# A decoder layer on one core: x is loaded turned and raw, the mean is taken out of the weights once, and GpSimd makes the two halves of x

## The reference, cut to what matters

```python
x   = x + self_attention(layernorm(x))        # x: 32 tiles of 128 tokens x 512, 16 heads of 32, RoPE, causal
x   = x + cross_attention(layernorm(x), ctx)  # queries and output through an int8 rounding per token
out = x + experts(layernorm(x))               # 64 experts, top 8, at most 128 rows each
# layernorm: (x - m) / sqrt(v + eps), over the 512 features, without gain or bias
# self attention: q = rope(xn @ Wq.T + bq), k likewise, v = xn @ Wv.T + bv; one 128 x 128 causal block per head
```

## Time and profile before

| | |
|---|---|
| median of 3 runs | 1784.66 us |
| profiled execution | 1771.08 us, its span 1769.2 us |
| PE, DVE, ACT, POOL busy | 84%, 66%, 55%, 38% of the span |
| mean granted TensorE clock | 0.918 of full speed |
| setup, up to the third body | 0 to 55 us |
| pipeline | 55 to some 1300 us |
| experts | some 1300 to 1769 us |

### The profile page before, as it was taken

How to read it: one execution, slowest core, us unless ns; L and a number is a source line. 1 busy time by engine, 2 the same in 40 slices (tenths; PEclk the granted TensorE clock), 3 DMA queues, 4 the chain that set the end, 5 groups by cost and what they waited for, 6 DMA issues and landing times.

```text
span 1769.2 us, 36416 instructions
## 1 busy us (share of the span) xinstructions
PE 1480.6 (84%) x11380; PEld 1111.3 (63%) x11380; DVE 1165.4 (66%) x3111; ACT 966.9 (55%) x3345; POOL 674.6 (38%) x654
## 2 busy tenths in 40 slices
PE   3699988888898888988888888888872988887895
PEld 2577766666666666766666666666651655555564
DVE  6788776777777777767767777776762444444453
ACT  3477665666666666666666666666661433333342
POOL 0114333333334333433333433333343355444465
PEclk9899999998999999999899999999985999999997
DMA  9752222221110101000001010100049799999974
GB/s 299 285 203 97 90 90 101 100 85 61 44 40 28 36 24 30 24 24 24 24 24 30 24 32 27 30 24 19 19 133 331 209 274 273 278 247 301 267 132 50
DMA packets 159930, 196.01 MB, mean 111 GB/s; under 512 B 39733, under 2 KB 121909, under 8 KB 159872
## 3 DMA queue, kind: packets, MB, share of 16 engines
q1 hardware_dynamic: 120960, 157.47, 27.1%
q0 software_dynamic: 38912, 37.87, 10.5%
HBM read 127.80 MB, written 130.29 MB: 146 GB/s over the span
## 4 chain that ended last, share of the span: by engine, by line
DVE 25%; PE 22%; DMA 20%; issue 14%; another core or an unknown queue 12%; ACT 5%; POOL 1%; DVEq 1%; SPq 0%; POOLq 0%
DMA out<-x,slots 18%; PE bank L513 11%; PE bank L519 4%; DVE small L1250 3%; ACT probs L980 3%; PE bank L541 3%; DVE xn L1269 2%; DVE wide_a L1319 2%; DVE small L1283 2%; PE bank L495 2%; DVE small L1273 1%; DVE x L1325 1%; DVE x L1450 1%; DVE wide_b L1493 1%
## 5 line engine op out<-in xcount | busy, mean ns | idle before, releaser
L980 ACT ACTIVATE probs<-bank,small 128x128 f32<-128x128 f32 x1024 | 364.2, 384 | 155.5 <-DVE small L1283 152.1
L1732 POOL TENSOR_TENSOR small<-small,half 128x1 f32<-128x1 f32 x96 | 54.6, 568 | 721.5 <-DVE small L1255 719.9
L1767 POOL DMA_INDIRECT routed<-row,slots x248 | 252.9, 1020 | 132.6 <-issue 72.9
L1836 POOL DMA_INDIRECT out<-x,slots x128 | 200.1, 1563 | 202.2 <-DMA out<-x,slots 148.5
L1283 DVE TENSOR_REDUCE small<-bank 128x4 f32<-128x512 f32 x256 | 166.9, 684 | 133.1 <-remote 125.1
L980 ACT ACTIVATION_READ_ACCUMULATOR probs<-bank,small 128x1 f32 x1024 | 228.6, 223 | 0.0
L974 ACT ACTIVATE probsT<-bank 128x512 f32<-128x512 f32 x256 | 144.0, 610 | 84.3 <-PE bank L541 81.9
L541 PE MATMUL bank<-idf,probs 128*128 128x128 f32 x1024 | 160.4, 293 | 3.9 <-ACT probs L980 3.9
L541 PEld LDWEIGHTS bank<-idf,probs 128*128 128x128 f32 x1024 | 130.5, 152 | 35.4 <-issue 6.5
L513 PE MATMUL bank<-w_q_hi,xT_hi 128*128 128x512 f32 x128 | 73.5, 575 | 79.3 <-DVE xatt L1299 35.7
L1687 DVE TENSOR_SCALAR slots<-pairs 128x1 uint32<-128x1 f32 x128 | 13.7, 149 | 189.3 <-DMA out<-x,slots 182.9
(11 more groups left out here) (242 smaller groups left out, 3982.5 us busy)
## 6 DMA issues: line engine op xcount, KB each, us to landing
w_gate_up<-in_w_gate SPq DMA_DIRECT2D x128, 192.0 KB
w_gate_up<-in_w_up SPq DMA_DIRECT2D x128, 192.0 KB
w_down<-in_w_down SPq DMA_DIRECT2D x128, 192.0 KB
routed<-empty_row SPq DMA_DIRECT2D x16, 1280.0 KB, 10.1
x_in<-in_x SPq DMA_DIRECT2D x32, 256.0 KB, 2.6
ctx_sb<-in_ctxT_in SPq DMA_DIRECT2D x32, 256.0 KB, 3.0
x_res<-in_x SPq DMA_DIRECT2D x32, 256.0 KB, 2.6
out<-x SPq DMA_DIRECT2D x32, 256.0 KB
```

The costliest lines, as they stand in the source:

```text
L980: last = act.activation(probs[:, g, j * P:(j + 1) * P], bank[:, b, j * P:(j + 1) * P], ACT.Exp, bias=negated[:, h:h + 1], **({"accum_out": ...
L1732: pool.tensor_tensor(c["r0"], c["v"], half[:, :], ALU.pow).then_inc(g_pow[kind], 1)
L1767: pool.indirect_dma_start(routed, bass.IndirectOffsetOnAxis(ap=slots_of(m)[:, k:k + 1], axis=0), row_of(m)[:, :], None, bounds_check=SLOTS ...
L1836: pool.indirect_dma_start(out.rearrange("b p (h c) -> (b p h) c", h=2), bass.IndirectOffsetOnAxis(ap=place_of[k % 2][:, half_:half_ + 1], ...
```

## The change

- A copy of x that is already turned (`xT_in`, each tile as four blocks of 128 x 128 side by side) is a further input. SP loads it for each tile into xn (`load_turned_x`), behind `load_x`, when GpSimd has split the tile before.
- GpSimd makes both halves: `turned_x_hi` casts xn to xT_hi and `turned_x_lo` subtracts. Both stand in its body behind the power of the cross norm and ahead of that of the self norm. They are of raw x, neither centred nor scaled.
- TensorE's `turn_x`, ScalarE's `x_hi`, VectorE's `self_normed` and `x_lo` are gone.
- The mean: for q, k and v TensorE adds up the 512 input rows of the staged weight with a matrix of ones (4 matmuls of 128 x 512 in fp32 each), and VectorE takes 1/512 of it from the staged weight (`centre`), before it is split. Done once, in the setup.
- The scale 1/sqrt(v + eps) of a token is applied behind the projections: to v by ScalarE in `copy_values`, to q and k by VectorE as a factor in the last step of `rotate`. The order in `rotate` is now: both sine products, the cosine product, their sum, and then sum times scale plus turned bias.
- The statistics and the scale are made one body later (for tile cur-1 and cur-2), so `load_x` waits for the statistics of the tile before and no longer for its normed x.

```diff
             def load_x(m):
-                reached(sp, d_ln["self"], m - 1, 7, 7)
+                reached(sp, d_ln["self"], m - 1, 6, 1)
                 sp.dma_start(x_in[:, :], x[tile(m)]).then_inc(s_x_in, 16)
+
+            def load_turned_x(m):
+                reached(sp, g_xT, m - 1, 2, 2)
+                sp.dma_start(xn[:, :], xT_in[tile(m)]).then_inc(s_xT, 16)
...
             def queries_a(m):
-                reached(pe, a_xT, m, 1, 1)
+                reached(pe, g_xT, m, 2, 1)
...
-                if has(cur - 1):
-                    turn_x(cur - 1)
...
-            pe.wait_ge(s_ident, 16)
+            pe.wait_ge(s_init, 2)
+            for n, b in enumerate((2, 3, 6)):
+                pe.wait_ge(s_wload[n], 16)
+                for t in range(KT):
+                    last = pe.matmul(bank[:, b, :], ones_f, STAGE[n][:, t, :], start=(t == 0), stop=(t == KT - 1))
+                last.then_inc(p_mean, 1)
...
-                copy(v_sb[:, :], bank[:, 6, :], e_v)
+                reached(act, d_ln["self"], m, 6, 6)
+                act.activation(v_sb[:, :], bank[:, 6, :], ACT.Copy, scale=ln["self"]["r"]).then_inc(e_v, 1)
...
-                act.wait_ge(s_wload[n % 4], 16 * (n // 4 + 1))
+                if n < 3:
+                    act.wait_ge(d_centred, n + 1)
+                else:
+                    act.wait_ge(s_wload[n % 4], 16 * (n // 4 + 1))
...
-                until(dve, d_rope, nth(m, 5, 2))
-                dve.tensor_tensor(rot, rot, turned_bias[:, :], ALU.add).then_inc(d_rope, 1)
+                until(dve, d_rope, nth(m, 5, 3))
+                dve.tensor_tensor(rot, rot, roped[:, :], ALU.add).then_inc(d_rope, 1)
                 until(dve, d_rope, nth(m, 5, 4))
-                dve.tensor_tensor(roped[:, :], roped[:, :], rot, ALU.add).then_inc(d_rope, 1)
+                dve.scalar_tensor_tensor(out=roped[:, :], in0=rot, scalar=ln["self"]["r"], in1=turned_bias[:, :],
+                                         op0=ALU.mult, op1=ALU.add).then_inc(d_rope, 1)
...
             body(1)
+            centre(0, 2)
+            centre(1, 3)
             weights_lo(0)
+            centre(2, 6)
             weights_lo(1)
...
+            def turned_x_hi(m):
+                reached(pool, s_xT, m, 16, 16)
+                reached(pool, p_v, m - 1, 3, 3)
+                apart(pool)
+                pool.tensor_copy(flat(xT_hi), xn[:, :]).then_inc(g_xT, 1)
+
+            def turned_x_lo(m):
+                reached(pool, g_xT, m, 2, 1)
+                pool.tensor_tensor(flat(xT_lo), xn[:, :], flat(xT_hi).bitcast(F32), ALU.subtract).then_inc(g_xT, 1)
```

More of the change, by code:

```diff
@@ L272, in layer @@
         d_ln = {k: sem(f"dve_ln_{k}") for k in ln}
-        d_xT, d_rope = sem("dve_xT"), sem("dve_rope")
+        LN_STEPS = {"self": 6, "cross": 7, "ffn": 7}
+        d_rope = sem("dve_rope")
+        d_centred = sem("weights_centred")
         d_max, d_norm, d_xmax = sem("dve_max"), sem("dve_normed_probs"), sem("dve_xmax")
@@ L407, in body @@
                     load_x(cur)
+                if has(cur):
+                    load_turned_x(cur)
                 if has(cur - 2):
@@ L432, in _ @@
                 fill(part)
+            load_turned_x(3)
             load_x(4)
@@ L437, in _ @@
             load_residual(2)
+            load_turned_x(4)
             for part in range(9, 12):
@@ L890, in turn_quantised_weights @@
                 last.then_inc(s_wT, 1)
+            pe.wait_ge(s_init, 2)
[4 more added lines that the diff above has]
+                last.then_inc(p_mean, 1)
+            body(1)
             pe.wait_ge(s_ident, 16)
-            body(1)
             pe.wait_ge(s_lo_dve, 3)
+            body(2)
             pe.wait_ge(s_init, N_INIT)
-            body(2)
             turn_quantised_weights()
@@ L1051, in copy_cross_keysT @@
                 last.then_inc(e_xkT, 1)
[L1053 to L1056, removed]
             def exp_1(m):
@@ L1442, in rotate @@
                     reached(dve, p_k, m, 3, 3)
+                    reached(dve, d_ln["self"], m, 6, 6)
                 rotate_pairs(4, m)
@@ L1527, in body @@
             def body(cur):
-                if has(cur - 1):
-                    self_rsqrt(cur - 1)
+                if has(cur - 2):
+                    self_rsqrt(cur - 2)
                 if has(cur - 5):
@@ L1557, in body @@
                     cross_max_3(cur - 4)
-                if has(cur - 1):
-                    self_normed(cur - 1)
                 if has(cur - 3):
@@ L1575, in body @@
                     shares(cur - 5)
-                if has(cur):
-                    self_statistics(cur)
+                if has(cur - 1):
+                    self_statistics(cur - 1)
                 if has(cur - 5):
@@ L1591, in body @@
                     cross_average(cur - 4)
-                if has(cur - 1):
-                    x_lo(cur - 1)
                 if has(cur - 2):
@@ L1616, in weights_lo, with centre @@
                                   ALU.subtract).then_inc(s_lo_dve, 1)
+            def centre(n, b):
+                dve.wait_ge(p_mean, n + 1)
+                dve.scalar_tensor_tensor(out=STAGE[n][:, :, :], in0=bank[:, b, :].unsqueeze(1).to_broadcast([P, KT, D]),
+                                         scalar=-1.0 / D, in1=STAGE[n][:, :, :],
+                                         op0=ALU.mult, op1=ALU.add).then_inc(d_centred, 1)
             body(1)
+            centre(0, 2)
+            centre(1, 3)
             weights_lo(0)
+            centre(2, 6)
             weights_lo(1)
@@ L1759, in self_power @@
             def self_power(m):
-                reached(pool, d_ln["self"], m, 7, 3)
+                reached(pool, d_ln["self"], m, 6, 3)
                 rsqrt("self")
@@ L1777, in bias_residual, with body @@
                 pool.tensor_tensor(x_res[:, :], x_res[:, :], att_bias[:, :], ALU.add).then_inc(g_res, 1)
-            def body(cur):
+            def body(cur, split=True):
                 if has(cur - 3):
@@ L1789, in body @@
                     cross_power(cur - 3)
-                if has(cur):
-                    self_power(cur)
+                if has(cur - 1) and split:
+                    turned_x_hi(cur - 1)
+                if has(cur - 1) and split:
+                    turned_x_lo(cur - 1)
+                if has(cur - 1):
+                    self_power(cur - 1)
                 if has(cur - 5):
@@ L1812, in _ @@
                 pool.tensor_copy(dst, src).then_inc(s_init, 1)
-            body(2)
+            body(2, split=False)
             pool.iota(row[:, D:ROW:2], pattern=[[0, E]], base=-P, channel_multiplier=1,
```

43 lines of the change are left out of this document (18 added, 25 removed).

## The result

The change is faster: 1690.29 us median of 4 (1683.42 to 1695.67) against 1785.41 (1784.63 to 1791.47), ratio 0.945 (95%: 0.943 to 0.947), 95 us less. Forecast was 1804, 19 more. What happened is rival B, which I had given 0.15 and 1700.

The account below looks back on a forecast made before the run. No engine is full: a chain bounds the body, a scatter stall, then nearly equal TensorE and VectorE limits. Profiled 1771.1 + 14.2 setup - 2.0 filling + 7.8 loop = 1791.1; carried to the median, 1804 us, range 1778 to 1832.

Parts of the forecast that it names:

- rival B: Loop: without transposes and their copy the late signal comes earlier, 26 x -4.0 = -104 us, to 1700; chance 0.15.
- the late signal at 598.40: Loop body: ScalarE takes the turned quantised x 11.5 us after the first scatter issue; removed work ahead costed at nothing.
- +7.8: Loop: 27 bodies, 6 to 32, each 0.29 us longer.
- its threshold: Rival B's sign in the loop: ScalarE's copy starts before the last scatter issue ends, under 10.3 us from the first.
- The setup: Ahead of the loop: turned load and mean delay x of the second tile by 13.1 us; +14.2 with turned x behind it.
- 1.1 - 2.0 = -0.9: Behind SP's load: turned x adds 0.4 for issue and 0.7 for transfer; filling, bodies 3 to 6, gives -2.
- VectorE's meeting with GpSimd: Loop body: cross-norm refinement held until GpSimd's subtraction ends, +0.66 us a body, bounds 0 and 1.27.
- A body's sum: Loop body: VectorE's savings -0.37 plus the refinement's wait +0.66 give +0.29 us, bounds -0.2 and +0.9.
- the total of +20.0: Whole kernel: setup +14.2, filling -2.0 and loop +7.8 us, profiled execution 1771.1 to 1791.1.
- Rival A: Loop: split misses VectorE's refinement, 27 x -0.21 = -5.7 us; sum +6.5, 1791; chance 0.20.
- rival C: Loop: loads of x and turned x lengthen the scatter's issues or come late, +1 us a body, 1831; chance 0.15.

Follow-up runs that it names:

- 3: Changed kernel with eight idle identity transposes ahead of TensorE's scores: 1553.56 us free (kernel before 1530.1), 1792.4 held (kernel before 1779.57).
- 9: Changed kernel with GpSimd's split moved ahead of the cross power and first tile's statistics ahead of the centring: 1778.01 us held (kernel before 1785.4), ratio 0.995.
- 6: Changed kernel without TensorE's column sums and the centring of q, k and v weights: 1546.4 us free (kernel before 1530.9).

## Why the prediction was wrong

- **The step that failed** is the one that cost the transposes, their copy and the low part at nothing, with the words that the late signal at 598.40 is one "which none of them makes". It isn't made by them, but its lateness depends on when TensorE reaches its scores, and both the missing transposes and the delay of the scatter moved that. In the held condition this was worth 3.3 us a body in the mean (40.46 to 37.19), -90.1 from the first to the 29th scatter, where the sum had +7.8. The copy's lateness was treated as a constant because 25 bodies showed it; they all had the same phase. The body of the earlier trace rows and the short one of the earlier trace rows were the evidence that it isn't, and 0.15 was too little for them.
- **Rival B** had the size (1700) and the sign, and its threshold held: the copy came before the last issue's end in 21 of 25 bodies. Its reason was only half right. It laid the delay to the signals and copies of the transposes; in 3 idle transposes without a signal or a copy bring the whole delay back, and in 9 a scatter that comes earlier does, with TensorE's work unchanged.
- **The setup** was right: +13.1 forecast for SP's load, 11.6 measured (33.1 against 21.5); +12.2 to the first scatter, 13.5 measured. Two misses offset each other in part: behind that load the sum had 1.1 - 2.0 = -0.9, the traces +1.9. The mean is nearly all of it (6).
- **VectorE's meeting with GpSimd** was right in kind, wrong in the victim and half the price. Forecast: +0.66 on the refinement L1264, at most 1.27. Measured: the cast at L1354, which stands ahead of it, took 1.26 in place of 0.17, L1351 took 0.42 in place of 0.18, +1.33 together, and the refinement kept its 0.16. The rule of the Trainium skill (SBUF — State Buffer, section "SBUF: two separate sides") has a VectorE operation in a fast mode wait out a GpSimd one that began first. The cast has one input and was shut out for the rest of the subtraction, which agrees with the rule if it ran in such a mode; no run here shows its mode.
- **A body's sum** of +0.29 and the total of +20.0 come near the free condition, where nothing hides behind the stall: +0.50 and +22.7. The mechanism of the sum is the one seen there: TensorE's limit went from 31.83 to 31.22, VectorE's chain with the meetings to 32.33. That the total is so close is partly luck: +12.1 from the first to the 29th scatter stands for +7.8, and 2.5 won at the end, which the sum had at nothing, make up for part of it.
- **Rival A** (no meeting) was 0.20 likely and is false; **rival C** (loads in the scatter's stretch) is false: in both conditions the loads stood there, and no wait in the loop is put down to a load.

Left open: what brings the held condition about (the same program, 40.7 or 31.8 us a body; chips 0, 6, 10, 11 and 14 of the record were free and 3 held, but number 2 stands for both, 1530.8 at one time and 1779.6 some eight minutes later), why the held signals come in groups, why one phase gives copies from 6.6 to 11.7 us, and what the pause alone is worth on the kernel before. For the last, its interrupted body, 36.7 us in place of 40.7, is the only sign.

## What to carry to other kernels

Where a trace shows waits put down to nothing ("remote") that end only when another engine's burst of DMA issues ends, expect their length to move with the phase between the two engines, and try a change's effect on that phase before its work. A gain from such a phase isn't the gain of the edit: run the kernel also where the wait is absent, and make the order explicit (one wait in the burst gave 90 us in one condition and cost 5 to 13 in the other). When a GpSimd operation is added, look for every VectorE operation that starts in its stretch, short casts included, and not only for those that are known to have met one.

## What the runs showed of the hardware that was not expected

- While GpSimd issued eight indirect DMAs (mostly 0.97 us each, 10.3 in all), TensorE's signals reached VectorE and ScalarE up to 7 us late in the held condition (made at 591.47, recorded at 598.37), in order, and all that were left within 1.5 us of the last issue's end. VectorE's and ScalarE's own signals were recorded 0.01 us behind their work in the same stretch. With GpSimd silent they were on time (562.29 and 564.40 above).
- With TensorE 0.23 us later against the first issue (0.56 to 0.33 ahead, by idle transposes) the copy came 4.3 us and the kernel 102 us later.
- In the free condition the same program shows none of it and is 255 us faster (1785 to 1530), 237 of them between the first and the 29th scatter (1127.3 to 890.5).
- A cast of 128 x 64 took 1.26 us instead of 0.17 beside a GpSimd subtraction that began 0.09 us ahead of it, and a one-input operation of the same size 0.42 instead of 0.18 beside a GpSimd cast that began 0.23 us ahead.
- The granted clock is 1.00 in bodies of the free condition and 0.92 to 0.95 in held ones, where TensorE stands still at each scatter.
